# A transformer layer on one core: score banks taken in two slots of two PSUM banks with one exponential per head and step, and two PSUM banks instead of three for the maxima

## The reference

```python
scale = DH ** (-0.5)
scores = jnp.einsum('bhtd,bhsd->bhts', q, k) / scale
if causal:
    scores = jnp.where(mask[None, None], scores, -jnp.inf)
attn = jax.nn.softmax(scores, axis=-1)
out = jnp.einsum('bhts,bhsd->bhtd', attn, v)
...
xn1 = _ln(x, g1, be1)
x = x + (_mha(xn1, xn1, ..., causal=True) @ W1 + b1)
xn2 = _ln(x, g2, be2)
x = x + (_mha(xn2, encoder_out, ..., causal=False) @ W2 + b2)
xn3 = _ln(x, g3, be3)
x = x + jax.nn.relu(xn3 @ Wf1 + bf1) @ Wf2 + bf2
```

## Time and profile before

| | us |
|---|---|
| median of 3 runs | 627.89 (627.78 to 629.59) |
| span of the profiled execution | 631.5 |
| TensorE busy in it | 504.7 |
| VectorE busy | 368.2 |
| ScalarE busy | 307.5 |
| self-attention, first score to last product | about 111 to 352 |
| cross-attention, first score to last product | about 410 to 500 |

### The profile page before, as it was taken

The page is one execution under the profiler, slowest core; times in us unless marked ns, Lnnn a source line. Parts: engine busy times, 40 slices in busy tenths (PEclk is TensorE's granted clock), DMA queues, the critical chain, the costliest instruction groups (busy, mean ns, idle before and its releaser), DMA issues.

```text
span 631.5 us, 8807 instructions
## 1 busy us (share of the span) xinstructions
PE 504.7 (80%) x3296; PEld 296.2 (47%) x3296; DVE 368.2 (58%) x695; ACT 307.5 (49%) x590; POOL 187.8 (30%) x276
## 2 busy tenths in 40 slices
PE   1775775999997999799988835669576757989887
PEld 0664452344443444344333333434222446988877
DVE  4887697678886788678532147645221763454430
ACT  3544020667765776477666502247443535253460
POOL 3788821131221132122132523305131350121200
PEclk9988697799999999899999969767555968999998
DMA  8138936007367335727260266978333212101001
GB/s 288 47 109 158 201 116 118 0 21 116 52 120 105 67 66 107 115 56 38 83 186 1 68 168 92 173 108 140 107 99 115 81 47 72 34 0 34 18 17 34
DMA packets 41930, 56.51 MB, mean 89 GB/s; under 512 B 12832, under 2 KB 27424, under 8 KB 41888
## 3 DMA queue, kind: packets, MB, share of 16 engines
q1 hardware_dynamic: 39584, 47.56, 38.1%
q10 hardware_dynamic: 2304, 8.39, 3.8%
HBM read 35.12 MB, written 20.42 MB: 88 GB/s over the span
## 4 chain that ended last, share of the span: by engine, by line
PE 44%; DMA 23%; DVE 15%; ACT 6%; SPq 5%; issue 3%; POOL 2%; ACTq 0%; DVEq 0%
PE ps L864 10%; PE ps L973 9%; PE ps L948 8%; PE ps L911 7%; DMA arena_h<-heads 6%; DMA stacks<-shift_t 6%; PE ps L1060 5%; DMA recips<-recip_rows 4%; DVE max_a L1141 4%; ACT arena_p L732 4%; DMA heads<-out_t 4%; DVE xn L1094 3%; SPq L409 2%; PE ps L933 2%; SPq L428 2%
## 5 line engine op out<-in xcount | busy, mean ns | idle before, releaser
L732 ACT ACTIVATE arena_p<-ps 128x512 f32<-128x512 f32 (+4 forms) x416 | 190.9, 541 | 129.5 <-PE ps L948 127.3
L1141 DVE TENSOR_REDUCE max_a<-ps 128x1 f32<-128x512 f32 (+4 forms) x280 | 159.6, 620 | 46.6 <-PE ps L911 34.0
L948 PE MATMUL ps<-stacks 99*128 99x512 bf16 (+2 forms) x448 | 149.9, 369 | 27.6 <-DMA stacks<-shift_t 22.5
L911 PE MATMUL ps<-stacks 96*128 96x77 bf16 (+4 forms) x640 | 146.2, 306 | 32.1 <-DVE max_a L1141 19.1
L911 PEld LDWEIGHTS ps<-stacks 96*128 96x128 bf16 x640 | 58.9, 111 | 97.5 <-DVE max_a L1141 45.5
L973 PE MATMUL ps<-arena_p,v_group 128*32 128x512 f32 (+4 forms) x896 | 94.1, 540 | 0.7 <-POOL arena_p L617 0.5
L617 POOL TENSOR_SCALAR_AFFINE_SELECT arena_p<-arena_p 128x512 f32<-128x512 f32 x64 | 41.0, 653 | 169.9 <-ACT arena_p L732 169.9
L948 PEld LDWEIGHTS ps<-stacks 99*128 99x128 bf16 (+1 forms) x448 | 45.6, 107 | 93.1 <-ACT arena_p L732 37.8
L1141 DVE TENSOR_REDUCE max_b<-ps 128x1 f32<-128x384 f32 (+3 forms) x88 | 52.5, 636 | 21.3 <-PE ps L915 21.3
L864 PE MATMUL ps<-wf2r,hid_r 128*128 128x256 f32 x384 | 49.9, 294 | 9.6 <-DVE hid_r L1254 9.6
L864 PEld LDWEIGHTS ps<-wf2r,hid_r 128*128 128x128 f32 x384 | 49.1, 202 | 10.7 <-DVE hid_r L1254 10.7
(11 more groups left out here) (68 smaller groups left out, 528.1 us busy)
## 6 DMA issues: line engine op xcount, KB each, us to landing
heads<-out_t ACTq DMA_DIRECT2D x16, 512.0 KB, 4.3
stacks<-q_parts SPq DMA_DIRECT2D x48, 128.0 KB, 5.2
stacks<-k_parts SPq DMA_DIRECT2D x48, 128.0 KB, 7.6
stacks<-qc_parts SPq DMA_DIRECT2D x48, 128.0 KB, 5.1
arena_h<-heads SPq DMA_DIRECT2D x8, 512.0 KB
recips<-recip_rows SPq DMA_DIRECT2D x8, 512.0 KB
q_parts<-parts SPq DMA_DIRECT2D x8, 384.0 KB, 2.5
k_parts<-parts SPq DMA_DIRECT2D x8, 384.0 KB, 2.6
```

Of the source, the lines that this page charges most:

```text
L732: nc.scalar.activation(probs[0:a.kp, a.probs_slot(g, ui), h, k * BANK:k * BANK + width], ps[0:a.kp, unit % S_BANKS, 0:width], ACT.Exp, sca ...
L911: ins = nc.tensor.matmul(m_bank(use)[:, o:o + w], q_stack[0:ROWS, g % a.nb, h, t * P:(t + 1) * P], k_rows(ROWS, g, h, s0, s0 + w), start=T ...
L948: ins = nc.tensor.matmul(ps[0:keys, unit % S_BANKS, lo - k * BANK:hi - k * BANK], k_rows(ROWS_S, g, h, i * P, i * P + keys), q_stack[:, g ...
L1141: nc.vector.tensor_reduce(dst, m_bank(use)[:, 0:nh * w].rearrange("p (h w) -> p h w", h=nh), AX.X, ALU.max).then_inc(s.max_read, 1)
```

## The change

Scores get two slots of two banks each (banks 0 to 3). A unit is now one head of a step, up to 1024 columns in one slot; it is one exponential. TensorE waits for the exponential of two units before. The matmuls stay as they are, split where a bank ends. The ring of the chunks has two banks (4 and 5) instead of three. The places of the transfers in the cross-attention are given in the new units.

```diff
-M_BANKS = 3
-S_BANKS = 3
+M_BANKS = 2
+S_SLOTS = 2
+S_BANKS = 2
...
-        self.units = [(ui, h, k) for ui, (_, width) in enumerate(self.steps)
-                      for h in range(GH) for k in range(-(-width // BANK))]
+        self.units = [(ui, h) for ui in range(len(self.steps)) for h in range(GH)]
...
-            self.moves = {"loaded": (2, 4), "inverted": (3, 0), "stored": (3, 1), "spread": (3, 3), "divided": (3, 6)}
+            self.moves = {"loaded": (2, 2), "inverted": (3, 0), "stored": (3, 0), "spread": (3, 1), "divided": (3, 3)}
...
     def unit_width(self, u):
-        ui, _, k = self.units[u]
-        return min(BANK, self.steps[ui][1] - k * BANK)
+        return self.steps[self.units[u][0]][1]
...
         def m_bank(use):
-            return ps[:, S_BANKS + use % M_BANKS, :]
+            return ps[:, S_SLOTS * S_BANKS + use % M_BANKS, :]
+
+        def s_slot(unit):
+            b = unit % S_SLOTS * S_BANKS
+            return ps[:, b:b + S_BANKS, :].rearrange("p b n -> p (b n)")
...
-                    nc.scalar.activation(probs[0:a.kp, a.probs_slot(g, ui), h, k * BANK:k * BANK + width],
-                                         ps[0:a.kp, unit % S_BANKS, 0:width], ACT.Exp, scale=SCALE)\
+                    nc.scalar.activation(probs[0:a.kp, a.probs_slot(g, ui), h, 0:width],
+                                         s_slot(unit)[0:a.kp, 0:width], ACT.Exp, scale=SCALE)\
...
-                    at_least(pe, s.exps, unit - S_BANKS + 1)
+                    at_least(pe, s.exps, unit - S_SLOTS + 1)
```

More of the change, by code:

```diff
@@ L98, in __init__ @@
         if causal:
-            ends = [max(u for u, (ui, _, _) in enumerate(self.units) if ui == step) for step in (2, 3, 3, 3, 5)]
+            ends = [max(u for u, (ui, _) in enumerate(self.units) if ui == step) for step in (2, 3, 3, 3, 5)]
             self.moves = dict(zip(("loaded", "inverted", "stored", "spread", "divided"), ((1, u) for u in ends)))
         else:
-            self.moves = {"loaded": (2, 4), "inverted": (3, 0), "stored": (3, 1), "spread": (3, 3), "divided": (3, 6)}
+            self.moves = {"loaded": (2, 2), "inverted": (3, 0), "stored": (3, 0), "spread": (3, 1), "divided": (3, 3)}
         self.order(lead, gap, rows)
@@ L133, in order @@
         for g in range(NG):
-            for u, (ui, h, k) in enumerate(self.units):
+            for u, (ui, _) in enumerate(self.units):
                 while stream and stream[0][0] <= g + unit_at[u] + lead:
@@ L725, in exp @@
                 def exp(g, u):
-                    ui, h, k = a.units[u]
+                    ui, h = a.units[u]
                     unit, width = len(a.units) * g + u, a.unit_width(u)
@@ L942, in score @@
                         pe.wait_ge(s.shift_in[g % a.nb], 16 * PARTS * (g // a.nb + 1))
-                    at_least(pe, s.exps, unit - S_BANKS + 1)
+                    at_least(pe, s.exps, unit - S_SLOTS + 1)
                     for i, q0, w, off in a.steps[ui][0]:
[L945 to L951, removed]
+                        for k in range(S_BANKS):
+                            lo, hi = max(off, k * BANK), min(off + w, (k + 1) * BANK)
+                            if lo < hi:
+                                keys = min(P, a.keys - i * P)
+                                ins = nc.tensor.matmul(s_slot(unit)[0:keys, lo:hi],
+                                                       k_rows(ROWS_S, g, h, i * P, i * P + keys),
+                                                       q_stack[:, g % a.nb, h, q0 + lo - off:q0 + hi - off],
+                                                       start=True, stop=True)
                     ins.then_inc(s.scores, 1)
```

## The result

The changed kernel takes 654.09 us in the median (653.24 to 655.58), the kernel before 628.74 in the same runs (627.78 to 632.33): 1.0405 times as long, 95% interval 1.0347 to 1.0463. That is 25.4 us more; the prediction had 14.3 more. One execution of the kernel before differs from the next by some us (622 to 636 over all its runs here), so stages are compared with a second trace of it, `before_again` (span 629.1). The span after is 651.5.

A forecast was written before the change was run, and what follows sets the result against it. DVE, with PE's products in its way, was taken to come close to setting the self-attention's pace. Terms 11.5 + 0.8 + 4 - 3 + 1 = +14.3 us on 627.9 gave 642 us; range 629 to 658.

The forecast's parts named there:

- rival C: Steady self-attention groups: longer waits bring PE to half clock for parts, each group losing 3 us more: 657 us; chance 9%.
- The forecast's own range: Whole kernel: 634 to 651 us, with the group's term from 1.5 to 3.6 and early from 0 to 6; chance 78%.
- Two maxima banks: Self-attention groups: DVE's gap behind each product grows by 0.48 us, a group by 2.9; 24 cycles make +11.5 us.
- What sets the pace: Steady self-attention group: DVE's 22.51 us of work and 5.44 us of gaps behind PE's products are the 28 us.
- The cover of the chain, and the shift: Self-attention groups with the transfer chain: DVE's loss, about 2.6 us, is covered; the shift is 0.4 us late, twice: +0.8.
- The early stage: Ahead of the first score: chunks at half clock and projection blocks lose cover with two banks: +4 us, from 0 to 6.
- The merged exponential: Both attentions: one exponential for a head saves at most 13 us on ACT, worth nothing where DVE paces.
- The end of the self-attention: 311 to 352 us, no chunks: cycles waiting for exponentials shrink, 4.2 to 3.6 for one: -3 us, from 0 to -5.
- The cross-attention: Its end hangs on transfers; the shift's bank has to be waited for, 0.3 us three times: +1, from -1 to +2.

The follow-up runs named there:

- the first experiment: The kernel before with two maxima banks instead of three, the freed bank idle, scores' three one-bank slots kept: 654.03 us, 1.0428.
- the second experiment: The changed kernel with the exponential of a unit issued as one instruction for each bank again, slots and order as they are: 656.74 us, 1.0486.
- the last cross-attention experiment: The kernel before with the whole change in the cross-attention alone, the self-attention keeping three and three banks: 634.98 us beside 631.28, 1.007.

## Why the prediction was right, and where its size was wrong

The direction was right for the main reason given, the lost bank, and the sum was 11 us short. The recorded range reached 658 us only through rival C's time. The forecast's own range ended at 651 us, so that 654 lies in the recorded one is luck: C's half clock in the steady groups did not come. The terms named for that own range in fact add up to 633 to 647.

By the traces (+22.4, where the forecast had +14.3) the groups are 4.2 us above their terms, the self-attention's end 3.4, the early stage 1.7 and the cross-attention 0.6. The rest of the kernel is 1.8 us shorter.

**Two maxima banks** (24 cycles by 0.48, +11.5). Right in its kind: the first experiment has the loss, the gaps behind the products grew by 3.0 us where 2.9 was forecast, and the backlog at a product's start was 0.49 us where 0.5 was forecast. Mis-sized, since a group grew by 4.65 us, beyond even the upper bound of 3.6. The step that failed is that the term counts the gaps behind the products and puts what lies between them at nothing. In the early stage's term the prediction had, for a chunk at full clock, 0.39 + 0.07 + 0.06 = 0.52 us from a reduction's end to the next filled bank, and called that covered by 0.60. But 0.60 is the distance of two starts, and a reduction ends 0.68 after its start. From its end to the time when DVE wants the bank again there are 2 x 0.60 - 0.68 = 0.52 us, and nothing is left over. Whatever PE does besides must then show as a wait; by this reading that is where the 1.6 us come from. The slots with their coarser order have a small part in it, for with the bank alone the group grew by 4.07 us, 2.75 of them behind the products.

**What sets the pace.** "DVE, with PE's products in its way, comes close to setting the pace" was wrong for the kernel before: half the columns to reduce gave 0.5 us of 28.0. The forecast came out on the right side since taking the bank makes the round trip the bound, whoever was it before.

**The cover of the chain, and the shift** (a pair of groups grows by one group's loss and 0.8). The cover was there: a pair took 61.7 us and takes 65.35, 3.65 more, where 2.9 + 0.8 = 3.7 was forecast. That the two agree is luck, for the parts differ: the plain group lost 4.65 and the chain's group gained 1.0. Its stall (3.6 us in the first trace of before where the prediction had 3.9, 3.2 in the second) is gone altogether, and so is the stretch at half clock behind it (a granted clock of 0.50 from 199.9 to 206.7 in the second trace; after, it is 1.00 from 124.78 to 385). The page shows the scores' wait for the shift's transfers in the whole kernel at 11.1 us, against 22.5 in the first trace of before and 23.9 in the second:

```profile
L952 PE MATMUL ps<-stacks 99*128 99x512 bf16 (+2 forms) x448 | 123.9, 364 | 17.4 <-DMA stacks<-shift_t 11.1
```

Over six groups, four times 4.65 less twice 1.05 are the 16.5 us, where 11.5 + 0.8 was forecast. From copy-out to the next pair's first score it was to stay at 27 us. It took 26.5 before (174.96 to 201.48) and takes 26.3 (187.40 to 213.66), now with no wait for the transfers at its end.

**The early stage** (+4, from 0 to 6): +5.7 by the first product of step 0, within the bounds, against the second trace of before. This term is the least certain one: against the same trace others with two banks in the self-attention stand at +4.3 to +9.1, and others with three at +0.9 to +2.8.

**The merged exponential** (nothing on the path): right, by the second experiment. Exponentials of 1024 columns last 1.024 us, 0.02 below the range given, whose upper end was read off a copy of 1024 columns and not off an exponential.

The Trainium skill (Perfetto Trace Analysis, Optimizing Scalar/DVE Operations) says that grouping into larger operations can improve throughput if the engine is saturated. ACT is not: it waits 12.7 of 32.67 us here, and no gain is seen, so the trace agrees.

**The end of the self-attention** (-3, from 0 to -5): +0.4. The group without chunks gained: from its first product to its last one's end 20.36 us before (328.71 to 349.07) and 19.64 after (352.01 to 371.65), so 0.7. The group ahead of it, which still has chunks, lost 1.1 (30.1 to 31.2). PE's products of steps 2 and 3 in the last group, before again and after:

```profile
338.99 1.50 PE L973 MATMUL ps<-arena_p,v_group 128*32 128x256 f32 x16
...
343.57 1.28 PE L973 MATMUL ps<-arena_p,v_group 128*32 128x128 f32 x16
```
```profile
361.66 1.50 PE L977 MATMUL ps<-arena_p,v_group 128*32 128x256 f32 x16
...
364.71 0.55 PE L952 MATMUL ps<-stacks 99*128 99x512 bf16 x2 [0.69 <-ACT arena_p L735]
...
365.52 0.55 PE L952 MATMUL ps<-stacks 99*128 99x512 bf16 x2 [0.26 <-ACT arena_p L735]
366.00 1.28 PE L977 MATMUL ps<-arena_p,v_group 128*32 128x128 f32 x16
```

The cycle shrank from 4.58 to 4.34, not from 4.2 to 3.6: with two slots PE waits for a whole head's exponential twice in a cycle, which the estimate of one wait left out. Four one-bank slots gain 3.4 us there against three, about what was written down for two of two.

**The cross-attention** (+1, from -1 to +2): the 0.3 us ahead of the shift's transposition are there (0.31 at 447.11). By traces it is +1.6 after, but by medians +3.7 with this part alone, above the bound. The clock goes with it, and the forecast had no term for that. Rival C looked for a falling clock in the steady groups, and there it kept 1.00; in the cross-attention the mean clock did fall, for a reason that stays open.

**What stays open.** The trace after accounts for 22.4 of the 25.4 us. The other 3 lie within what one execution of either kernel differs from the next. The clock is the likeliest carrier, which is not shown: of the executions of before beside the last cross-attention experiment, the one at a mean granted clock of 0.899 took 627.49 us and the one at 0.873 took 635.08. Two maxima banks in the self-attention alone cost 22.0 us by the medians (649.42 less 627.46) and the whole change in the cross-attention 3.7, 25.7 together.

## What to carry to other kernels

For a reader without gaps, a ring of banks would have had to cover the whole round trip of this kernel: the reader's full duration (0.68 us), the reaction (0.07), and the writer until the bank is readable (0.39 to 0.45), plus the longest block in which the writer does something else (1.85). Work that sum out with durations of completion, not with the pace of back-to-back instructions. Two banks (2 x 0.60 us) only just meet the trip itself, and nothing is left for the block. Three (1.8 us) do not cover all of it either, but there the gaps cost next to nothing, as DVE was not the bound. Before taking a buffer for a saving on an engine that waits anyway, look which engine it waits for: the saving becomes a longer wait, and the lost buffer is paid in full. An engine whose gaps and work together fill the time need not be the bound: shorten the suspected work by half in an experiment and see, and look first whether it is in the chain that ended last.

## What the runs showed of the hardware that was not expected

- A PSUM bank came back to TensorE 0.75 us after the start of VectorE's 512-column reduction of it (0.07 after its end), while the next reduction had started at 0.60.
- Cutting 16 fp32 matmuls into two blocks of 8, with bf16 matmuls between, took 2.00 us of PE in place of 1.86.
- With the change in the cross-attention alone the mean granted clock of the executions was 0.874 beside 0.886, and their time 3.7 us longer. The short stops of PE that came with it (0.31 us) are not what it takes: with two maxima banks alone, and no idle row after 420.25 us, the stretch had 0.56 too.
